# Two of a shared expert's eight units moved behind the routed blocks, beside the final sums, and the routed weights' conversions spread over the first six

## The reference

```python
def _swiglu(x, wg, wu, wd):
    return jax.nn.silu(x @ wg) * (x @ wu) @ wd
probs = jax.nn.softmax(x @ Wr, axis=-1)                 # 8 experts
routing_weights, selected = jax.lax.top_k(probs, 2)
moe_out = sum over the two chosen experts of routing weight * _swiglu(x, Wg[e], Wu[e], Wd[e])   # F = 176
shared = jax.nn.sigmoid(x @ Wsg) * _swiglu(x, Sg, Su, Sd)                                       # FS = 704
x = _layernorm(x + moe_out + shared)
```

## Time and profile before

| | |
|---|---|
| time, median of 3 (range) | 854.47 us (854.35 to 861.86) |
| time of the profiled execution | 853.95 us |
| its span | 852.2 us |
| mean granted TensorE clock | 0.901 |
| busy share: TensorE, VectorE, ScalarE, GpSimd | 83%, 68%, 54%, 31% |

### The profile page before, as it was taken

The page is one execution under the profiler, slowest core; times in us unless marked ns, Lnnn a source line. Parts: engine busy times, 40 slices in busy tenths (PEclk is TensorE's granted clock), DMA queues, the critical chain, the costliest instruction groups (busy, mean ns, idle before and its releaser), DMA issues.

```text
span 852.2 us, 17828 instructions
## 1 busy us (share of the span) xinstructions
PE 709.5 (83%) x5074; PEld 632.9 (74%) x5075; DVE 578.8 (68%) x1512; ACT 457.8 (54%) x1155; POOL 262.4 (31%) x400
## 2 busy tenths in 40 slices
PE   5997699777665989999999999986669998999910
PEld 5886478644335989999989999976569998888800
DVE  5887587767887476777867888865465455555536
ACT  5231466467851257777766887853433334555513
POOL 3332200233438000211111111121784401555545
PEclk9897799958976999999998999997679999999955
DMA  9920000000003876666664655610441101333252
GB/s 303 350 71 0 1 1 1 1 1 2 0 10 136 250 244 175 179 191 194 193 198 134 199 158 152 163 39 7 140 129 60 61 19 45 101 98 104 81 196 100
DMA packets 66483, 95.56 MB, mean 112 GB/s; under 512 B 11390, under 2 KB 52992, under 8 KB 66304
## 3 DMA queue, kind: packets, MB, share of 16 engines
q1 hardware_dynamic: 63024, 86.51, 34.4%
q0 software_dynamic: 3408, 8.43, 2.8%
HBM read 62.45 MB, written 33.36 MB: 112 GB/s over the span
## 4 chain that ended last, share of the span: by engine, by line
PE 56%; issue 16%; DVE 13%; DMA 5%; POOL 5%; ACT 2%; SPq 2%; DVEq 0%; POOLq 0%; ACTq 0%
PE bank L1818 12%; PE bank L1804 6%; PE bank L1894 6%; PE bank L1955 5%; PE bank L1549 4%; PE bank L1909 3%; PE bank L1793 3%; PE bank L1787 3%; PE bank L1979 3%; PE bank L1834 2%; PE bank L1943 2%; DMA xg<-X,idx 1%; SPq L474 1%; DVE X L1061 1%; PE bank L1583 1%
## 5 line engine op out<-in xcount | busy, mean ns | idle before, releaser
L1818 PE MATMUL bank<-f_mem,late_mem 128*128 128x68 f32 (+3 forms) x1024 | 129.3, 270 | 0.0
L1818 PEld LDWEIGHTS bank<-f_mem,late_mem 128*128 128x128 f32 x1024 | 125.9, 194 | 0.8 <-issue 0.7
L590 POOL TENSOR_TENSOR rstd<-var,power 128x2 f32<-128x2 f32 (+1 forms) x64 | 43.8, 684 | 214.7 <-DVE var L1054 209.2
L1308 DVE TENSOR_REDUCE smax<-bank 128x4 f32<-128x512 f32 x128 | 88.0, 690 | 23.0 <-PE bank L1793 21.7
L899 ACT ACTIVATE late_mem<-bank 128x512 f32<-128x512 f32 x128 | 77.8, 608 | 22.6 <-PE bank L1804 20.4
L1804 PE MATMUL bank<-ident,late_mem 128*128 128x128 f32 x512 | 77.5, 274 | 3.1 <-ACT late_mem L889 1.9
L889 ACT ACTIVATE late_mem<-bank,smax 128x128 f32<-128x128 f32 x256 | 73.5, 383 | 11.4 <-DVE smax L1308 11.4
L1793 PE MATMUL bank<-kz,qs 128*128 128x256 f32 x256 | 75.4, 377 | 0.0
L1804 PEld LDWEIGHTS bank<-ident,late_mem 128*128 128x128 f32 x512 | 59.3, 141 | 4.0 <-ACT late_mem L889 2.5
L883 ACT ACTIVATE late_mem<-late_mem 128x512 f32<-128x512 f32 x64 | 41.0, 641 | 24.5 <-DVE late_mem L1315 23.6
L1894 PE MATMUL bank<-x_hi,w_hi 128*128 128x256 f32 x176 | 52.8, 300 | 1.0 <-DVE x_lo L1372 1.0
(11 more groups left out here) (280 smaller groups left out, 2095.7 us busy)
## 6 DMA issues: line engine op xcount, KB each, us to landing
qs<-q_D SPq DMA_DIRECT2D x64, 128.0 KB, 2.7
kz<-k_D SPq DMA_DIRECT2D x128, 64.0 KB, 2.6
qs<-q_E SPq DMA_DIRECT2D x64, 128.0 KB, 2.7
kz<-k_E SPq DMA_DIRECT2D x128, 64.0 KB, 2.5
xg<-f_mem SPq DMA_DIRECT2D x1, 5031.0 KB, 22.8
late_mem<-xg SPq DMA_DIRECT2D x39, 129.0 KB, 2.0
q_D<-stage_d SPq DMA_DIRECT2D x8, 512.0 KB, 2.9
k_D<-stage_d SPq DMA_DIRECT2D x8, 512.0 KB, 3.9
```

What stands on the lines that cost most here:

```text
L590: gp.tensor_tensor(rstd[:, slot, 0:n], var[:, slot, 0:n], power[:, 0:n], ALU.pow).then_inc(sem("ln_rstd"), 1)
L1308: ve.tensor_reduce(smax[:, g, :], v, axis=AX.X, op=ALU.max, negate=g not in SUBS).then_inc(sem("core_max"), 1)
L1818: ins = mm(bank[6][:, h * (DH + 1):to * (DH + 1)], spt[:, g, i, :], vf[:, slot, h:to, :].rearrange("p h d -> p (h d)"), start=True, stop=True)
```

## The change

- `EARLY = NU - 2`: units 0 to 5 run ahead of the routed blocks; 6 and 7 run behind them, on all three engines. Unit 6's x is prepared in unit 5 already. TensorE starts them when the last block is transposed, gated and copied out (`R_xl`, `R_h`, `R_y`).
- The final sums are interleaved: VectorE does sum 0 to 5 (`finish`) at offsets 4, 5, 7, 8, 10, 11 of the twelve late chunks (`TAIL_AT`) and sums 6 and 7 behind them; ScalarE normalises units 0 to 3 between late chunks and 4 to 7 behind them. GpSimd's first addition of unit `t` now waits for `F_sum >= t + 1`.
- The twelve conversions go to chunks 6, 8, 11, 13, 16, ... 33 (`ROUTE_AT`), one per 2.5 chunks, in place of chunks 0 to 11. `route_low` moves from GpSimd to VectorE, one chunk behind `route_high`. GpSimd's scatters stand alone. SyncE waits for all twelve subtractions before the block loads.

```diff
+EARLY = NU - 2
+TAIL_AT = {4: 0, 5: 1, 7: 2, 8: 3, 10: 4, 11: 5}
+ROUTE_AT = {6 + 5 * k // 2: k for k in range(NRC)}
...
+            sp_.wait_ge(sem("F_rl"), NRC)
             sp_.wait_ge(sem("scattered"), 16 * 2 * B)
             pipelined(sp_, NBLK, [(0, load_block)], 2, 2)
...
-            def route_low(c):
-                _, (hi, lo), at, _, n = route_chunk(c)
-                pool.wait_ge(sem("F_rh"), c + 1)
-                gp.tensor_tensor(lo[:, at:at + n], r_in[:, c % 2, 0:n], hi[:, at:at + n], ALU.subtract).then_inc(sem("F_rl"), 1)
...
-                    if k == 0 and b < NRC:
-                        route_low(b)
...
+                    pool.wait_ge(sem("F_sum"), t + 1)
                     gp.tensor_tensor(rows(acc, t), rows(acc, t), rows(back[:, 0, :], t), ALU.add).then_inc(sem("F_half"), 1)
...
-            for c in chunks(0, NU):
+            for c in chunks(0, EARLY):
                 t, f = divmod(c, NF)
                 silu(c)
                 if c > 0:
                     hid_high(c - 1)
-                if c < NRC:
-                    route_high(c)
-                if f == 2 and t + 1 < NU:
+                if c in ROUTE_AT:
+                    route_high(ROUTE_AT[c])
+                if f == 2:
                     x_high(t + 1)
-            hid_high(NU * NF - 1)
+            hid_high(EARLY * NF - 1)
...
-            for t in range(NU):
+            act.wait_ge(sem("R_hp"), NBLK)
+            act.wait_ge(sem("R_h"), NBLK)
+            first = EARLY * NF
+            for c in chunks(EARLY, NU):
+                t, f = divmod(c, NF)
+                silu(c)
+                if c > first:
+                    hid_high(c - 1)
+                if f == 2 and t + 1 < NU:
+                    x_high(t + 1)
+                if TAIL_AT.get(c - 1 - first, 0) > 0:
+                    normalize(TAIL_AT[c - 1 - first] - 1)
+            hid_high(NU * NF - 1)
+            for t in range(EARLY - 2, NU):
                 normalize(t)
...
+            def route_low(c):
+                _, (hi, lo), at, _, n = route_chunk(c)
+                dve.wait_ge(sem("F_rh"), c + 1)
+                ve.tensor_tensor(lo[:, at:at + n], r_in[:, c % 2, 0:n], hi[:, at:at + n], ALU.subtract
+                                 ).then_inc(sem("F_rl"), 1)
...
+                if c - 1 in ROUTE_AT:
+                    route_low(ROUTE_AT[c - 1])
+            hid_low(EARLY * NF - 1)
+            add_shared(EARLY - 1)
...
-            for t in range(NU + 1):
+            def finish(t):
                 if t < NU:
                     dve.wait_ge(sem("F_half"), t + 1)
...
+            first = EARLY * NF
+            for c in chunks(EARLY, NU):
+                t, f = divmod(c, NF)
+                gate(c)
+                if c > first:
+                    hid_low(c - 1)
+                if f == 3 and t + 1 < NU:
+                    x_low(t + 1)
+                if f == 3 and t > EARLY:
+                    add_shared(t - 1)
+                if c - first in TAIL_AT:
+                    finish(TAIL_AT[c - first])
+            hid_low(NU * NF - 1)
+            add_shared(NU - 1)
+            for t in range(EARLY, NU + 1):
+                finish(t)
...
+            def shared(t0, t1):
+                for c in chunks(t0, t1):
+                    products(c)
+                    if c == 1:
+                        count()
+                    if c >= t0 * NF + 2:
+                        down(c - 2)
+                down(t1 * NF - 2)
+                down(t1 * NF - 1)
+
+            shared(0, EARLY)
...
-                    pe.wait_ge(sem("F_sum"), NU)
+                    pe.wait_ge(sem("F_sum"), EARLY)
...
+            pe.wait_ge(sem("R_xl"), NBLK)
+            pe.wait_ge(sem("R_h"), NBLK)
+            pe.wait_ge(sem("R_y"), NBLK)
+            shared(EARLY, NU)
```

More of the change, by code:

```diff
@@ L1473, in _ @@
                     table_blocks()
-                if f == 3 and t + 1 < NU:
+                if f == 3:
                     x_low(t + 1)
@@ L1477, in _ @@
                     add_shared(t - 1)
-            hid_low(NU * NF - 1)
-            add_shared(NU - 1)
+                if c - 1 in ROUTE_AT:
+                    route_low(ROUTE_AT[c - 1])
+            hid_low(EARLY * NF - 1)
+            add_shared(EARLY - 1)
             def block_meta(i, slot):
```

## The result

The changed kernel takes 829.21 us (median of 4 runs, 826.17 to 834.66) against 855.75 us; the ratio is 0.9678, 95% interval 0.9642 to 0.9713. The forecast was 819.4 us with a range of 810 to 831. The profiled execution took 827.95 us, its span is 826.2 us, so it took 8.6 us more than the sum said.

The account below looks back on a forecast made before the run. Bounds: load waits stalling TensorE in the early units, TensorE in the routed blocks, the VectorE-GpSimd round in the final sums. Sum: 853.95 - 44.7 + 3 + 7.1 = 819.4 us, range 810 to 831.

Parts of the forecast that it names:

- Step 1: Six units ahead of the routed blocks, conversions spread: no load waits, 12.54 us each, TensorE ready at about 664.
- Step 2: Scatters without arithmetic between them, paced like the old second pass, end last at 666.4; block 2's load earlier: -44.7 us.
- the likeliest case: The forecast's main sum, 819.4 us, with scatters ending last before the routed blocks; 50 in 100.
- Rival C: Scattering: with weight loads beside it every turn takes 5.4 us, scatters end at 680.8, +14.4, 834 us; 11 in 100.
- Step 3: Head of the routed blocks: TensorE's idle gap brings the half clock, +3 us, bounds 0 and 5.
- Step 4: Tail, reload start to end: VectorE does gates, subtractions and final sums; grows from 35.2 to 42.3 us, +7.1 us.
- Rival B: Tail: TensorE at half clock after stalls ends some 5 us later than VectorE, 825 us; 16 in 100.
- A: Before the routed blocks: scatters end at 662.4, TensorE's 664 decides, no long gap, about 812.5 us; 14 in 100.
- D: Six units: spreading does nothing, loads stay late, stalls and slow clock return, 842 us; 4 in 100.
- E: Routed blocks: the gap leaves TensorE at half clock throughout, slower than before, 893 us for all 39; 3 in 100.

Follow-up runs that it names:

- the part alone: Conversions spread as in the changed kernel, but all eight units ahead of the routed blocks and final sums where they stood before: 834.65 us, ratio 0.9752.
- the kernel with the filler: The changed kernel with 70 unread products on TensorE between unit 5 and the routed blocks: 829.76 us, ratio 0.9692.

## Why the prediction was right, and where its steps were off

**What bounds the kernel before: right.** The load waits in front of Silu made the stalls. Without them TensorE is busy 40.03 of 41.48 us; the part alone gives 0.9752, 21 us, and back in place the stalls return.

**Step 1, six units at 12.54 us: right.** The last addition starts at 666.50, 71.5 us behind the first scatter; 664 and 593.7 give 70.3. VectorE's twelve subtractions fit. They took 0.89 and 1.22 us (0.94 and 1.37 forecast). The last one ended at 663.6, not near 658; here the scatters hid that, with four in flight the block loads waited for it.

**Step 2, the scatters: the mechanism right, the size 5.4 us short.** That they end last and open a gap was the likeliest case, and it happened: removing the wait gave 11 us. The failed sentence is "That is what the second pass already is". The second pass of the kernel before runs when the weights' loads are over (the last starts at 630); in the changed kernel the first pass and the start of the second have the loads beside them, whose place the change itself moved. Without loads the passes take 71.35 us, the forecast's 72.7. The shortfall lies in the first pass, 41.5 us against 36.0. The second took 36.6, as forecast, though four loads of 512 KB start in its first half: three of the turns there took 4.0 to 4.4 us and one 6.5, so a load beside a turn does not always slow it. Rival C (a turn of 5.4 us) came true for seven of the sixteen turns (5.1 to 6.5), though the 5.45 it was taken from ran without loads. By the Trainium skill, DMA: Bandwidth & Descriptors, Anatomy of one DMA, a DMA of 132 KB takes an estimated 2.3 us to land (2.0 plus its bytes over 436 GB/s). The scatters' median is 2.7 us in both kernels, and GpSimd, its own time over, waited 2.4 to 3.9 us more for a pair beside the weight loads; the measurement decides.

**Step 3, the clock: the sign right, the size about half.** The stage from block 2's load was 105.4 us against 106.2 forecast; the +3 us for the half clock measured 1.4 as the mean over kernels, 2.2 against the one execution of before. That a short gap keeps the clock, which was taken from the 2.39 us stall before, does not hold. In the kernel without loads a gap of 2.13 us, behind another of 1.07, was followed by a mean clock of 0.63 over 9 us:

```profile
670.00:679.00 9.00, 8.46 (x39) 7.35 (x39) 4.14 (x19) 3.25 (x10) 0.19 (x1) 0.63 0.19 49
```

In the kernel with doubled subtractions one stall of 2.35 us in a busy stretch was enough; a product takes 0.28 us ahead of it and 0.41 behind:

```profile
670.44 0.28 PE L1930 MATMUL bank<-x_hi,w_lo 128*128 128x256 f32 x1
...
676.15 0.58 PE L1945 MATMUL bank<-w_hi,hid_hi 128*128 128x256 f32 x1 [2.35 <-DVE hid_lo L1399]
676.53 0.41 PE L1945 MATMUL bank<-w_lo,hid_hi 128*128 128x256 f32 x1
```

So in this range the length of a gap does not say by itself what the clock will do.

**Step 4, the tail: the mechanism right, 2.3 us short, and nearer in the total than in its parts.** VectorE's queue sets it. The split of unit 7's x was missing from the sum, and GpSimd's first two additions fell on it and on a subtraction: the first sum started 8.4 us behind the reload and not 6.8 (+1.6). Where they fall varies from execution to execution: in the kernel with the filler, whose tail is the same code, the split ran ahead of them in 0.68 us, the first sum started 6.85 us behind the reload, and the tail took 42.7 us, the forecast's 42.3. From the first sum to the last subtraction it took 22.4 us, 21.7 forecast (+0.7), but the single steps do not bear the working out: from sum to sum 2.8, 5.3, 4.2, 4.2 and 2.8 us, where it had 2.95 for a sum with one chunk, 4.45 with two, 2.95, 5.33 with two and unit 6's additions, and 2.95. Errors of up to 1.2 us cancelled; that the total came out is in part luck. The last subtraction to sum 7 took 2.95 and not 2.2, the last down products being at half clock (+0.8). The end behind it was 0.6 shorter. Rival B, the half clock in the tail, was a matter of degree: 0.50 for 2.9 us and again in the last down products. The cost is an estimate, 2 us: VectorE's wait of 1.2 us for Silu at 801.17, and those 0.8. By the Trainium skill, SBUF: State Buffer, Who interferes with whom, a VectorE instruction with two inputs in SBUF contends with a GpSimd one that reads SBUF; the 0.42 us and 0.68 us of these subtractions and sums once GpSimd adds nothing agree with it.

**Rivals.** A (scatters not last) did not happen in the changed kernel. Made to happen, its profiled execution took 816.01 us and not 812.5: 1.4 us more up to block 2's load and 2.0 more in the tail. (The 4.25 us that A calls the shortest turn isn't quite: the same pass has 4.18.) D and E fell: no stall above 1.1 us inside the six units, and the clock was back within 9 us.

**The range.** 829.21 us lies inside 810 to 831, 1.8 us from its upper end, and one of the four executions took 834.66. The change brought 26.5 us where 34.5 were forecast, and of the five rows of the landmarks all but one came out slower than forecast. The range held because it had been drawn wide enough for rival B, not because the likeliest case came out at its figure.

## What to carry to other kernels

When work is moved away from an engine, look at what the engine that ran beside it will be waiting for: a chain of transfers that was hidden by 29 us here came out by 7 us and swallowed a quarter of what both edits could give. Price a transfer from a stretch that has the traffic it will have after the change, and if its completion is awaited in turn, try keeping one more in flight first. Work that fills an idle engine at the end costs the engine that consumes it: the first unit moved cost 2.8 us of tail, the second 5 to 8.

## What the runs showed of the hardware

- Scatters of 128 rows of 1032 bytes, two in flight, take mostly 4.0 to 4.7 us a turn alone, with one or two turns of 5.4 to 5.9 in a pass of eight. Beside loads of 352 KB they take 4.2 to 6.5 us, mostly over 5, with the DMA engines busy only 37% of the time; beside loads of 512 KB two turns of the changed kernel stayed at 4.3 and 4.4. With four in flight, a turn takes 2.5 to 3.4 us with the same loads, one in each second pass excepted (4.4 to 4.6); 2.5 is GpSimd's own time (1.26 us each).
- TensorE's granted clock went to half behind a gap of 2.13 us that followed another of 1.07 us, behind one of 2.35 us in a busy stretch, and in the tail of the changed kernel (0.50 from 797.80) just behind one of 1.50. It did not behind one of 2.39 us in the kernel before, nor behind stalls of 1.50 in the tail of the kernel with the filler.
- The start of the same stage varied by 6 us between executions of kernels whose code up to there is the same, and the same tail took 42.7 to 45.7 us. A difference of a few us between two kernels is read more safely from the stage that the edit touches than from the end, and from several executions.
